# Re-listing the work around two convergence checks and ahead of the experts, in a fused sparsemax-attention and slot-mixture kernel

## The reference, cut to what matters

```python
x = query                                  # (2, 2048, 256)
# first layer: sparsemax attention over 32 patterns, 16 heads
k = key_param @ Wk + bk; v = k @ Wv + bv   # 32 rows each
z = scale * einsum(heads(norm(x) @ Wq + bq), heads(k))   # (2, 16, 2048, 32)
A = max(z - tau, 0)                        # tau so that each row of A sums to 1
x = x + norm((A @ v) @ Wo + bo)
# second layer: 16 slots, one expert per slot
y = norm(x)
o = q + mha(slots q, keys y, values y)     # softmax over all tokens of the batch
o = o + silu(h@W1+b1) * silu(h@Wg+bg) @ W2 + b2    # h = norm(o) * g + b, 16 experts of 3 x 1 MB
x = x + norm(mha(queries y, keys o, values o))
```

## Time and profile before

| | us |
|---|---|
| median of 3 runs (lowest, highest) | 473.92 (473.73, 474.47) |
| the profiled execution's own time | 473.89 |
| its span, first to last instruction | 472.2 |
| busy: PE / DVE / ACT / POOL | 395.3 / 313.0 / 226.1 / 149.4 |

### The profile page before, as it was taken

One profiled execution on the slowest core, in us unless ns is written; L12 is line 12 of the kernel. 1 busy time (PEld: TensorE's weight loads), 2 busy tenths in 40 slices (PEclk: granted clock), 3 DMA queues, 4 the chain that ended last, 5 costly groups with the idle time before them and its releaser, 6 DMA issues. The chain is left out here.

```text
span 472.2 us, 6963 instructions
## 1 busy us (share of the span) xinstructions
PE 395.3 (84%) x2085; PEld 245.2 (52%) x2091; DVE 313.0 (66%) x1189; ACT 226.1 (48%) x412; POOL 149.4 (32%) x243
## 2 busy tenths in 40 slices
PE   3886576778977988899999899989998379999983
PEld 3542232234544444565766675734444137888872
DVE  3699999986999998477415245243333124989996
ACT  2235558565685889677773744200000001356671
POOL 4104735655567453333032010010000000335353
PEclk9997988788999999899999999999999989999997
DMA  4384111010101054637717867759999999901215
GB/s 149 90 279 128 40 45 29 16 44 2 44 1 46 1 168 165 228 114 243 269 70 289 310 191 285 258 208 393 400 385 403 383 383 337 341 1 46 73 62 178
DMA packets 44319, 83.78 MB, mean 177 GB/s; under 512 B 1911, under 2 KB 36349, under 8 KB 39933
## 3 DMA queue, kind: packets, MB, share of 16 engines
q1 hardware_dynamic: 43224, 82.15, 49.5%
q10 hardware_dynamic: 1060, 1.22, 0.9%
HBM read 70.78 MB, written 12.58 MB: 177 GB/s over the span
## 5 line engine op out<-in xcount | busy, mean ns | idle before, releaser
L1087 PE MATMUL bank<-Wz,yT 128*128 128x512 f32 x128 | 70.8, 705 | 25.9 <-DVE top L1666 23.3
L1087 PEld LDWEIGHTS bank<-Wz,yT 128*128 128x128 f32 x128 | 28.0, 227 | 61.6 <-issue 50.4
L1666 DVE MAX8 top<-bank 128x8 f32<-128x32 f32 x512 | 51.5, 179 | 1.9 <-ACT arena L762 1.7
L1023 ACT ACTIVATE d<-d 128x32 f32<-128x32 f32 x16 | 3.7, 229 | 86.9 <-DVE d L2045 86.9
L595 POOL TENSOR_SCALAR veps<-mv 128x4 f32<-128x4 f32 x24 | 5.9, 246 | 99.8 <-DVE mv L1594 71.7
L703 POOL TENSOR_TENSOR work<-work 128x512 f32<-128x512 f32 x16 | 16.6, 1061 | 64.8 <-DVE work L2120 64.8
L1120 PE MATMUL bank<-aWo,hoT 128*128 128x256 f32 x128 | 36.0, 404 | 0.1
L1154 PE MATMUL bank<-arena,Wd 128*128 128x512 f32 x64 | 29.3, 600 | 3.8 <-ACT arena L825 3.8
L1183 PE MATMUL bank<-d,work 128*128 128x256 f32 x128 | 30.3, 382 | 1.9 <-ACT d L853 1.9
L1526 PE MATMUL bank<-scr,work 128*128 128x256 f32 x128 | 29.1, 381 | 1.6 <-ACT work L1036 1.6
L1502 PE MATMUL bank<-scr,arena 128*128 128x256 f32 x128 | 28.9, 380 | 0.0
(11 more groups left out here) (272 smaller groups left out, 881.4 us busy)
## 6 DMA issues: line engine op xcount, KB each, us to landing
arena<-in_L_ffn_e_W_dram SPq DMA_DIRECT2D x14, 1024.0 KB, 11.0
scr<-in_L_ffn_e_W_dram SPq DMA_DIRECT2D x7, 1024.0 KB, 13.5
x<-in_L_ffn_e_W_dram SPq DMA_DIRECT2D x5, 1024.0 KB, 4.8
x<-in_L_ffn_e_Wg_dram SPq DMA_DIRECT2D x5, 1024.0 KB, 10.2
xin<-in_L_attn_query_dram SPq DMA_DIRECT2D x8, 512.0 KB, 4.0
x<-in_L_attn_query_dram SPq DMA_DIRECT2D x1, 4096.0 KB, 16.6
out_dram<-x SPq DMA_DIRECT2D x8, 512.0 KB, 5.4
away_dram<-arena SPq DMA_DIRECT2D x8, 512.0 KB, 8.6
```

What stands on the lines that cost most here:

```text
L1087: mm = pe.matmul(bZ[t % 2][:, :], yT[:, c, t * P:(t + 1) * P], Wz[:, c, :], start=(c == 0), stop=(c == C - 1))
L1666: mx = v.max(top[:, h * TG + t, :], bZ[t % 2][:, h * NS:(h + 1) * NS])
```

## The change

Two orders of the lists are joined and a few pieces of them are moved:

- First check: DVE's `first_statistics` of group 6 goes from behind the check to between its comparison and its maximum; PE's fillers (10, now 8) go from ahead of `sum_moved(0)` to behind it; POOL's `subtract(4)` no longer waits for `settled` (the correction loop of batch 0 gets a scratch tile in `work`).
- Groups 5 and 6: `join_add` goes inside `settle`, ahead of its last addition, and `join_statistics` behind it; before, both stood ahead of `settle`. POOL's `lower` goes ahead of `roots(2, ...)`.
- ACT: the sign passes of groups 5, 6 and 7 write into a tile that is no longer read (`unread`, over `y`) instead of `above`, so that `clamp` and `mark` of group 7 can stand ahead of `signs(6)`; `norm_o(2)` and the copies of group 1's slot scores go behind the last signs.
- PE: `slot_scores(1)` goes behind all of `heads_of(3)`, one half on each side of `sum_moved(1)`, in place of 5 fillers.
- Batch 1's stretch: group 2's and 3's second norm, transposes and slot scores one step of n later.
- Ahead of the experts: `second_norm(6)`, `second_norm(7)`, `turn_norm(7)` and `slot_scores(7)` earlier, the exponentials of groups 4 and 5 in one piece, 9 fillers left out, `to_slots(0, 2)` and `to_slots(0, 3)` behind `mix_p(12)` and `mix_p(13)`.

The core of the diff (the rest moves DVE's `group_maximum` and `merge` and ACT's calls in the same way):

```diff
@@ gpsimd
             values(0)
-            pool.wait_ge(settled, 1)
...
+                if i < NG - 1:
+                    lower(i, 1)
                 if g > 0:
                     roots(2, g - 1)
                 if i < NG - 1:
-                    lower(i, 1)
                     values(g + 1, range(2, TG))
@@ scalar
+                if isinstance(i, int) and i > GB:
+
+                    act.wait_ge(yT_ps, NG)
+                    act.wait_ge(signed, i)
+                table = unread if isinstance(i, int) and i > GB else above[:, :]
...
-            second_norm(1)
-            take_a(12)
-            signs(6, 1)
-            take_o(11)
-            put_norm(1)
-
-            clamp(7, range(1))
-            take_a(13)
-            take_h(12)
-            clamp(7, range(1, 2))
-            mark(7)
-            put_slot_scores(1)
+            take_a(12)
+            second_norm(1)
+            clamp(7, range(1))
+            take_o(11)
+            take_a(13)
+            clamp(7, range(1, 2))
+            mark(7)
+            take_h(12)
+            put_norm(1)
             take_a(14)
             take_h(13)
             take_o(12)
+            signs(6, 1)
...
-            exponential_of_part(False, 0)
             put_probabilities(7)
-            exponential_of_part(False, 1)
+            for m in range(2):
+                exponential_of_part(False, m)
+            norm_o(7)
             put_probabilities(8)
             put_probabilities(9)
-            second_norm(6)
-            norm_o(7)
             put_norm(6)
@@ tensor
-            keep_clock(7, 10)
             sum_moved(0)
+            keep_clock(7, 8)
...
-            heads_of(3, range(1))
+            heads_of(3, range(2))
             turn_norm(1)
-            heads_of(3, range(1, 2))
-            slot_scores(1)
             heads_of(3, range(2, TG + 2))
+            slot_scores(1, range(1))
             sum_moved(1)
-            keep_clock(2, 5)
+            slot_scores(1, range(1, 2))
@@ vector
+                if joined >= 0:
+                    join_add(joined)
                 v.wait_ge(newton, at + 3)
                 v.tensor_tensor(tauf[:, :], tau[:, :], rcnt[:, :], ALU.add).then_inc(tau_ready, 1)
...
                 v.tensor_tensor(tot[:, 1, 0:n], tot[:, 1, 0:n], tot[:, 0, 0:n], ALU.not_equal).then_inc(compared, 1)
+                if b == 0:
+                    first_statistics(GB + 2)
...
                 count(i, 1, False)
+                settle(i, 1, False, g - 1)
                 if g > 0:
-                    join(g - 1)
-                settle(i, 1, False)
+                    join_statistics(g - 1)
```

More of the change, by code:

```diff
@@ L773, in mark, with last_signs @@
                 act.activation(above[:, :], d[:, :], ACT.Sign).then_inc(marked, 1)
-            def last_signs():
-                for u in range(2):
+            unread = y[:, :, :].rearrange("p t d -> p (t d)").bitcast(BF16)
+            def last_signs(halves=range(2)):
+                for u in halves:
+                    act.wait_ge(signed, NG - 1)
                     act.wait_ge(lowered, NG + u)
-                    act.activation(above[:, u * 1024:(u + 1) * 1024].rearrange("p (h t s) -> p h t s", h=NH // 2, t=TG),
+                    act.activation(unread[:, u * 1024:(u + 1) * 1024].rearrange("p (h t s) -> p h t s", h=NH // 2, t=TG),
                                    scr[1][:, u * NH // 2:(u + 1) * NH // 2, KT - TG:KT, :], ACT.Sign, bias=tiny[:, 0:1],
@@ L924, in _ @@
             take_o(6)
+            put_scores(7, 1, range(1))
             second_norm(0)
-            put_scores(7, 1, range(2))
+            put_scores(7, 1, range(1, 2))
             take_o(7)
             take_a(8)
+            clamp(6, range(1))
             put_norm(0)
-            clamp(6)
-            signs(5, 1)
+            clamp(6, range(1, 2))
             take_a(9)
             take_h(8)
+            signs(5, 1)
             norm_o(1)
@@ L963, in _ @@
             take_o(13)
+            last_signs(range(1))
             take_h(15)
+            take_o(14)
+            last_signs(range(1, 2))
+            take_o(15)
             norm_o(2)
-            take_o(14)
-            last_signs()
-            take_o(15)
+            put_slot_scores(1)
             for n in range(KT, 2 * KT + 2):
@@ L1147, in turn_norm, with slot_scores @@
                 mm.then_inc(ynT_ps, 1)
-            def slot_scores(g):
+            def slot_scores(g, halves=range(2)):
                 pe.wait_ge(ynT_sb, 2 * (g + 1))
-                for m in range(2):
+                for m in halves:
                     for c in range(C):
@@ L1354, in _ @@
             slot_scores(6)
+            turn_norm(7)
             turn_p(11)
             mix_p(10)
+            slot_scores(7)
             mix_p(11)
             to_slots(0, 0)
[L1359 to L1368, removed]
             pe.wait_ge(q_in, 16)
@@ L1377, in _ @@
             mm.then_inc(turned, 1)
+            to_slots(0, 1)
+            pe.wait_ge(part, 2)
+            for m in range(2):
+                for c in range(C):
+                    mm = pe.matmul(psH[:, m * P:(m + 1) * P], gT[:, c, m, :], dWv[:, c, m * P:(m + 1) * P],
+                                   start=(c == 0), stop=(c == C - 1))
+            mm.then_inc(part_ps, 1)
             pe.wait_ge(pT_sb, 12)
-            keep_clock(5, 9)
             turn_p(12)
@@ L1383, in _ @@
             mix_p(12)
+            to_slots(0, 2)
+            turn_p(14)
+            mix_p(13)
             to_slots(0, 3)
-            for n in range(13, 15):
+            for n in range(14, 15):
                 turn_p(n + 1)
@@ L1771, in check @@
                 with v.If(v.value_load(flagi[0:1, 0:1]) > 0):
+                    left_over = (work[:, 4096:6144].rearrange("p (h t s) -> p h t s", h=NH, t=TG), d3)[b]
                     with v.Fori(0, GB) as g:
@@ L1971, in _ @@
             finish_last()
-            join_add(2)
             check(1)
-            join_statistics(2)
+            join(2)
+            v.wait_ge(rst[1], 3)
             output_statistics(3)
@@ L1994, in _ @@
                     own(v.tensor_tensor(sq[:, :], sq[:, :], dbo, ALU.add))
-                if n in (23, 28):
-                    join(4 if n == 23 else 5)
+                if n in (24, 28):
+                    join(4 if n == 24 else 5)
                 if n == 32:
```

69 lines of the change are left out of this document (36 added, 33 removed).

## The result

| | before | after |
|---|---|---|
| median of 11 runs each, us | 474.04 (471.52 to 474.55) | 470.11 (467.23 to 472.11) |
| ratio, 95% interval | | 0.9936 [0.9917, 0.9956] |
| profiled execution, its span | 473.89, 472.2 | 470.11, 468.3 |

The change makes the kernel 0.64% faster (0.44 to 0.83%), by the ratio some 3.0 us, by the medians 3.9. The forecast was 471.4 us, 2.5 won against the profiled execution of before. The profiled execution of after is its own median.

What follows compares the result with a forecast made beforehand. The work before the experts was taken as the bound, since the DMA stream was not yet saturated. 2.4 won by batch 1, less 1.2 for the clock, plus 1.3 ahead of the experts gave 2.5: 471.4 us, range 469.6 to 473.6.

Steps and rivals of the forecast that it cites:

- The rule that the time before the experts moves the end: Expert weight stream: not yet saturated when the experts start, so time won before them moves the end by as much.
- rival 3: At the end: the DMA stream, not the experts' start, sets it, so little is left, 473.6 to 473.9; chance 0.09.
- First check: First check, groups 4 to 6: flag 0.85 earlier, next maxima 2.6 earlier, `count(4)` 1.65 earlier.
- Rival 2: First check: POOL's `subtract(4)` gets ahead of DVE's comparison, taking off 1.1 to 2.9, 472.5 to 474.3; chance 0.13.
- Scans: DVE scans of groups 5 and 6: no longer held up by POOL's `lower`, 1.4 instead of 2.23, 0.83 won each.
- ACT's stretch: Group 7, first clamp to last sign on ACT: list still takes 14.0, with 0.15 lost at the clamp.
- The clock: PE idling around `turn_norm(1)`, 173.5 to 177: the clock falls and `take_o(12)` is late, costing 1.2.
- Rival 1: PE around `turn_norm(1)`: the clock stays up, 3.7 won, 470.2; chance 0.30.
- Rival 4: PE from 177: low clock lasts until the second check's sum, so the kernel is slower, 474.9 to 479; chance 0.10.
- Sum and flag: Second check: half of `slot_scores(1)` delays the sum, then flag and transposes follow; first `mix` of batch 1 2.4 earlier.
- Ahead of the experts: PE's list before the experts: 5.5 of waits and fillers go, 4.2 of new waits come, 1.3 won.
- The sum: Whole kernel: 1.2 up to batch 1 plus 1.3 ahead of the experts, 2.5 won, 471.4.

Runs made afterwards that it cites:

- `bridge`: Changed kernel with 4 fillers ahead of `turn_norm(1)` and 13 behind it; ratio to before 0.9885.
- `first_alone`: Kernel before with only the edit of the first check; ratio to before 1.0003.
- `lists_undone`: Changed kernel with POOL's `lower` back behind `roots(2)` and DVE's `join` back ahead of `settle` in groups 4 to 6; ratio to before 0.9965.
- `tail_undone`: Changed kernel with the order of before put back on PE, ACT and DVE in the stretch ahead of the experts; ratio to before 0.9926.
- `sum_first`: Changed kernel with both halves of `slot_scores(1)` behind the sum of the second check; ratio to before 0.9963.
- `first_third`: Kernel before with the edit of the first check and 9 fillers ahead of the last expert; ratio to before 0.9967.
- `all_three`: Changed kernel with fillers around `turn_norm(1)`, two places ahead of the experts turned round, and 9 fillers ahead of the last expert; 468.86 us, ratio to before 0.9898.
- `late_slots`: Changed kernel with fillers around `turn_norm(1)`, `to_slots(0, 3)` behind `mix_p(14)`, and 9 fillers ahead of the last expert; 466.88 us, ratio to before 0.9861.

## Why the prediction held, step by step

- **The rule that the time before the experts moves the end.** Right. In the 14 traces the first product of the last expert comes 72.8 to 73.5 behind the first expert product, whether that is early or late; rival 3 is out. What I missed is that the stretch behind it can give 0 to 2.4 back, 0.8 net here.
- **First check.** Right in kind, too small. I gave 1.65 at `count(4)` against 2.41. Of the missing 0.76, 0.52 is the flag: I let it wait 0.3 for `subtract(4)` and it did not, and 0.2 was small terms. The other 0.24 is probably the clock, which I had not thought of here: the stretch from 112 to 116 is at 1.00 instead of 0.65, and a `mix` takes 0.65 instead of 1.12. No run tests that by itself. Rival 2 did not occur, by 0.03 us.
- **Scans.** Right place, right reason, size 1.0 instead of 0.83 each. Undoing it brought the 2.21 back. Of the small operations of `roots` that I feared, one is held up itself (0.69 for 0.20). `tau(7)` was 4.6 earlier, not 3.15: 2.4 from the first check, 2.0 from the scans, and 0.2 in small terms, where I had taken off 0.15 for the clamps of group 6.
- **ACT's stretch.** 14.8 from clamp to last sign instead of 14.0, 1.0 of it from the low clock (`take_o(12)` waits 1.38 for `project(12)`). What my text did not weigh is the whole of this new order: from the end of `tau(7)` to the first `mix` of batch 1 it takes 22.09, and 21.10 in `bridge` with the clock up, against 20.73 before and 20.85 in `first_alone`. In return the clock stays up around the second check, where `first_alone` lost 0.84. No run puts the order of group 7 alone back, so whether it is worth having is open.
- **The clock.** Forecast right: it fell. I took 1.2, fillers gave back 1.0. Rival 1's premise, that it stays up, is wrong, though by the other errors its 470.2 is nearer to the median than my 471.4. Rival 4 did not occur: low for some 3 us. It is near, though: in `lists_undone` the two stretches 176 to 184 stood at 0.66 and 0.50.
- **Sum and flag.** The chain sum, flag, transposes was the wrong bound. The half of `slot_scores(1)` delays the sum by 1.4 and costs nothing, since PE needs that time for the same work anyway. That step, and not only its size, was wrong in my text.
- **Ahead of the experts.** 1.1 against 1.3. Waits of 1.35, 0.78 and 1.21 where I had 1.45, 0.7 and 1.3.
- **The sum.** 4.4 at the experts against 2.5 forecast: 1.45 more at `tau(7)`, 0.6 more from there to batch 1 (I let 1.95 go on the way, 1.35 went), 0.2 less ahead of the experts; then 0.3 came back in the stream and 0.8 more than in before was lost behind the third wait, which leaves the 3.9. The forecast has no such loss. That the end came nearer to it than the 4.4 at the experts was luck.

## What to carry to other kernels

Cost a check or flag by asking what the waiting engine has to do anyway: put its own work around it, and the flag's latency can cost nothing, as it did at the second check here. When two engines hold each other up, what counts is who starts first, so check edits of such an order in pairs: `join` moved alone was slower than neither moved. Where gains are under 1%, compare positions inside traces from a common point, since start and end of the program here vary by as much as the gain.

## What the runs showed of the hardware

- A DVE scan (128x512, bf16 in) and a `lower` of POOL (3.64, two SBUF inputs) don't run together: from group 2 on a scan started beside a `lower` 52 times in the 14 traces, and took 1.54 to 3.62 by where it started but ended 1.07 to 1.09 behind the end of the `lower` each time. It takes 1.23 where no `lower` runs. A short operation is less clear: POOL's `rstd` (128x4, 1.04 long, two inputs) still ran for the first 0.46 of such a scan in after, without the scan taking longer, while the next one (L600) took 0.69 instead of 0.20 and ended with the scan. The Trainium skill ("SBUF — State Buffer", section "SBUF: two separate sides") names the lock; the traces agree for the scan beside a `lower`. They show no hold-up of the statistics (1.40 for 4, as elsewhere), of the maxima or of the flag's copy beside `subtract(4)`.
- The granted clock fell behind `turn_norm(1)` in each trace with the gap of 3.3 to 4.9, and in none with it filled; behind the first wait for expert weights, of 3.44 to 3.60, it fell in some traces and stayed up in others (before, `tail_undone`). The Trainium skill ("TensorE: Matmul & The Clock Gate", section "Why this matters for your kernels") warns of such gaps; the traces agree for the first place and not always for the second. Behind the last expert it fell in five of the 14 traces (after, `first_alone`, `sum_first`, `first_third`, `all_three`). The kernels differ little there, and filling one wait did not prevent it.
- A low clock cost nothing where the DMA stream is the bound: in `late_slots` it stood at 0.50 from 364 to 372, and the experts still took their 73.1.
